# First attention: query and key projections leave PSUM through ScalarE, the rotary products move to GpSimd, and the DMA queue's order changes

## The chip, the cores and the metric

The kernel runs on 1 core of a Trainium2 chip. The metric is the device time of one execution in microseconds (us), the median of several runs. The engines are TensorE (PE in the profile, its weight loads PEld), VectorE (DVE), ScalarE (ACT), GpSimd (POOL) and SyncE (SP, which here only issues DMAs). They run side by side and wait for one another by semaphores.

## The reference

Eight batches of 128 x 256 go through a cross attention, a mixture-of-experts layer, a second cross attention and a low-rank expert layer. The change is in the first attention alone. `b` is 8, `d_model` 128, `n` 256; there are 16 heads of 8 channels.

```python
def apply_cached_rotary_emb(freqs, t):
    return t * freqs[0] + rotate_half(t) * freqs[1]
q = proj(Wq, bq, query).reshape(b, HD, H, n)     # proj: W @ x + bias
k = proj(Wk, bk, key).reshape(b, HD, H, n)
v = proj(Wv, bv, value).reshape(b, HD, H, n)
q = jnp.transpose(apply_cached_rotary_emb(encoding, jnp.transpose(q, (0, 2, 3, 1))), (0, 3, 1, 2))
k = ... the same for k
scores = jnp.einsum('bdhn,bdhm->bhnm', q, k) / np.float32(np.sqrt(HD))
prob = jax.nn.softmax(scores, axis=-1)
x = jnp.einsum('bhnm,bdhm->bdhn', prob, v)
out = jnp.einsum('oi,bin->bon', Wm, x.reshape(b, d_model, n)) + bm[None, :, None]
```

## The kernel before

**Rounds.** The first attention takes one round for each batch b, 0 to 7. A round has eight pairs of heads and two spots for each, spots 0 to 15. At the even spots TensorE makes the scores of the next pair (L679) and, for a batch further on, the same scores once more for their row maxima (L658); spots 3, 7, 11 and 15 multiply probabilities by values (`pv`, L694). Three things of later batches are woven in: the maxima of batch b+1 (pairs 2 to 7 at spots 0 to 10) and of batch b+2 (pairs 0 and 1, spots 12 and 14), the projections of batch b+3 (`q` at spot 1, `k` at spot 5), and the values of b+1 (spot 9).

**The ring.** Projections, maxima, transposed maxima (`maxT`) and values all go through three PSUM banks, used in turn. A use of a bank waits until the use three before it has been taken out. All are taken out by VectorE, in the program's order, which counts `misc_free` up. A pair's maxima need two banks and two VectorE reduces (L1535).

**Projection to scores.** `project` (L643) writes W x and the rotated W x into one bank. VectorE's `factors` (L1524) adds the bias and multiplies by the rotary table, once for each half, into `rope_ab`. GpSimd adds the halves into `qk` (`add_factors`, L454). Scores need full precision from bf16 products, so `qk` is split into three bf16 parts: ScalarE casts the first (`first_parts`, L1140), GpSimd subtracts it (L457), ScalarE casts the second (`second_parts`, L1144), GpSimd subtracts that into the third (`third`, L460). SP writes the parts replicated into a DRAM scratch (`parts_to_dram`, six DMAs), and reads them back as stacks `qstk` and `kstk` (`stack_from_dram`, four DMAs), of which there are three sets.

**Maxima to scores.** When four pairs of a batch (a half) have their maxima, GpSimd negates them and splits them in three (`negate`, six small instructions, L1364 to L1368), TensorE transposes them (`maxT`, L666), VectorE copies them out (L1539), and SP writes them as rows into `qstk` (`rows_at`, L533). The scores of that half wait for these rows. `maxT` stands at spots 6 and 14, ahead of a `pv`, so TensorE, which works in order, holds everything behind it until `negate` is done.

**GpSimd's round**, in order: `divide` of batch b-1; `negate` of half 0; then for batch b+3 the add, the first subtraction, `normalize` of b+4 (L1378), the third part; then `negate` of half 1. In rounds 5 and 6 there is no batch b+3, and no projection, add or parts. ScalarE also does the exponentials (L1133), one for each pair, and in rounds 1 to 4 issues two weight DMAs at pair 1; in rounds 5 and 6 it issues zero fills of 1 MB there.

## Time and profile before

| | us |
|---|---|
| median of 3 runs | 404.87 (400.6 to 405.14) |
| the profiled execution, its own time | 402.56 |
| span in its trace | 400.8 |
| VectorE busy over the span | 290.7 (73%) |
| TensorE busy | 297.2 (74%) |
| ScalarE busy | 166.5 (42%) |
| GpSimd busy | 100.1 (25%) |

The span runs from the first to the last instruction; the rest of an execution's time lies around it. Busy shares are averages over stages with different limits, so the first attention (about 21 to 146 us of the span) has to be read by its rounds. A row of a timeline gives the start, the time to the end of the last instruction in it, the engine, the line, what is written from what, how many instructions were merged, and in brackets the idle time ahead of it with what ended it.

### The profile page before, as it was taken

The numbers are of one execution on the slowest core, as the hardware profiler recorded it, in microseconds if no ns is written. First come the engines' busy times: TensorE is split into PE (matmuls) and PEld (weight loads), VectorE is DVE, ScalarE is ACT, GpSimd is POOL, SyncE is SP. The second block draws the span as 40 slices with busy tenths as digits, with TensorE's granted clock in tenths as the row PEclk, the third lists the DMA queues.
The fourth block names the chain that finished last, engine by engine and source line by source line (L and its number), as shares of the span: only waits on it lengthen the run. The fifth ranks groups of instructions, "written<-read, shape, count | busy, mean of one in ns | idle before, by whom it ended". The sixth has DMA issues, their size and how long they took to land.

```text
span 400.8 us, 7274 instructions
## 1 busy us (share of the span) xinstructions
PE 297.2 (74%) x2650; PEld 187.0 (47%) x2650; DVE 290.7 (73%) x771; ACT 166.5 (42%) x264; POOL 100.1 (25%) x201
## 2 busy tenths in 40 slices
PE   4156978888777668999969998044857696776894
PEld 3122444444434425876648997022534454452453
DVE  6977789989988866769134674275878978776894
ACT  1103376476575565163335664011644545350101
POOL 1234246346343222007701120645000001000000
PEclk9855699999999999599998999555888969698999
DMA  7593447857859451002262775625466564510011
GB/s 249 164 267 101 131 115 218 271 139 222 263 162 265 151 201 61 2 0 90 101 186 79 229 227 194 184 79 144 138 180 182 152 202 141 167 43 0 2 52 52
DMA packets 76387, 58.19 MB, mean 145 GB/s; under 512 B 5056, under 2 KB 73152, under 8 KB 76352
## 3 DMA queue, kind: packets, MB, share of 16 engines
q1 hardware_dynamic: 66688, 42.68, 35.6%
q10 hardware_dynamic: 8128, 10.85, 8.7%
q0 software_dynamic: 1536, 4.20, 3.3%
q8 instruction: 21, 0.34, 0.4%
q14 instruction: 14, 0.11, 0.1%
HBM read 32.87 MB, written 24.64 MB: 143 GB/s over the span
## 4 chain that ended last, share of the span: by engine, by line
PE 37%; DVE 26%; DMA 11%; issue 10%; SPq 5%; ACT 4%; POOL 4%; another core or an unknown queue 1%; DVEq 0%; POOLq 0%
DVE mx L1535 8%; DMA stack_scratch<-parts 5%; PE psum L986 4%; PE psum L694 4%; PE psum L998 3%; PE psum L643 3%; PE psum L856 2%; PE psum L797 2%; PE psum L658 2%; DVE rope_ab L1524 2%; PE psum L811 2%; PE psum L974 2%; PE psum L679 2%; SPq L487 1%; PE psum L1092 1%
## 5 line engine op out<-in xcount | busy, mean ns | idle before, releaser
L1535 DVE TENSOR_REDUCE mx<-psum 128x2 f32<-128x512 f32 x128 | 81.1, 682 | 14.3 <-PE psum L658 12.9
L1133 ACT ACTIVATE prob<-psum 128x1024 f32<-128x1024 f32 x64 | 63.8, 1022 | 41.9 <-PE psum L679 41.9
L1307 ACT ACTIVATE prob<-psum 128x1024 f32<-128x1024 f32 x32 | 32.5, 1023 | 28.0 <-PE psum L946 28.0
L658 PE MATMUL psum<-kstk,qstk 64*128 64x256 bf16 x256 | 27.7, 299 | 22.0 <-DVE mx L1535 12.3
L694 PE MATMUL psum<-prob,vt 128*32 128x256 f32 x512 | 35.9, 392 | 5.3 <-ACT prob L1133 4.2
L460 POOL TENSOR_TENSOR parts<-qk_rest,parts 128x256 bf16<-128x256 f32 (+1 forms) x15 | 13.5, 901 | 66.8 <-ACT parts L1282 63.5
L658 PEld LDWEIGHTS psum<-kstk,qstk 64*128 64x128 bf16 x256 | 9.9, 99 | 35.4 <-DVE mx L1535 24.0
L679 PE MATMUL psum<-qstk,kstk 64*128 64x256 bf16 x256 | 25.2, 282 | 0.3 <-DMA qstk<-mT 0.2
L694 PEld LDWEIGHTS psum<-prob,vt 128*32 128x32 f32 x512 | 16.3, 110 | 13.6 <-ACT prob L1133 6.0
L946 PE MATMUL psum<-qstk,kstk 64*128 64x128 bf16 x256 | 14.2, 240 | 10.8 <-issue 9.8
L962 PE MATMUL psum<-prob,vt 128*32 128x128 f32 x512 | 21.7, 292 | 0.2 <-ACT prob L1307 0.2
L784 PE MATMUL psum<-eye,xn 128*128 128x128 f32 x32 | 8.0, 340 | 15.9 <-DVE xn L1807 11.1
L986 PE MATMUL psum<-xnT,qstk 128*128 128x128 f32 x124 | 17.9, 290 | 2.3 <-DVE xnT L1776 2.2
L1447 POOL DMA_INDIRECT wup<-sorted_y,slots x16 | 15.3, 958 | 15.8 <-issue 15.6
L1076 PE MATMUL psum<-wd,xnT 128*128 128x512 f32 x32 | 16.2, 654 | 3.9 <-DVE xall L1852 3.9
L679 PEld LDWEIGHTS psum<-qstk,kstk 64*128 64x128 bf16 x256 | 8.5, 95 | 20.8 <-issue 13.0
L986 PEld LDWEIGHTS psum<-xnT,qstk 128*128 128x128 f32 x124 | 16.4, 205 | 3.0 <-DVE xnT L1776 2.4
L925 PE MATMUL psum<-wc,xT 128*128 128x256 f32 x32 | 13.7, 571 | 4.8 <-DVE qk_rest L1846 4.2
L946 PEld LDWEIGHTS psum<-qstk,kstk 64*128 64x128 bf16 x256 | 8.4, 103 | 18.6 <-issue 12.7
L1140 ACT CAST parts<-qk 128x512 bf16<-128x512 f32 x8 | 4.9, 617 | 28.8 <-POOL qk L454 17.3
L811 PE MATMUL psum<-wdn,act 128*128 128x256 f32 x64 | 15.2, 381 | 1.5 <-ACT act L1204 1.5
L1524 DVE SCALAR_TENSOR_TENSOR rope_ab<-psum,cols,rope 128x256 f32<-128x256 f32 x32 | 13.6, 469 | 3.4 <-PE psum L643 3.2
(244 smaller groups left out, 621.6 us busy)
## 6 DMA issues: line engine op xcount, KB each, us to landing
qstk<-stack_scratch SPq DMA_DIRECT2D x32, 256.0 KB, 4.2
kstk<-stack_scratch SPq DMA_DIRECT2D x30, 256.0 KB, 4.6
stack_scratch<-parts SPq DMA_DIRECT2D x23, 192.0 KB, 2.1
prob<-sorted_x SPq DMA_DIRECT2D x15, 256.0 KB, 3.2
stack_scratch<-parts SPq DMA_DIRECT2D x25, 128.0 KB, 2.1
sorted_x<-zero_row ACTq DMA_DIRECT2D x3, 1024.0 KB, 5.0
wup<-in_wup ACTq DMA_DIRECT2D x4, 640.0 KB, 4.9
wdn<-in_wdn ACTq DMA_DIRECT2D x4, 640.0 KB, 6.3
```

Of the source, the lines that this page charges most:

```text
L658: last = nc.tensor.matmul(banks[s][:, nb * D:(nb + 1) * D], qstk[par][rows, pair, nb * P:(nb + 1) * P], kstk[par][rows, pair, :], start=Tr ...
L679: last = nc.tensor.matmul(exp_buf(k)[:, s, mb * D:(mb + 1) * D], kstk[b % SETS][rows, k, mb * P:(mb + 1) * P], qstk[b % SETS][rows, k, :], ...
L694: last = nc.tensor.matmul(pv_bank(1)[32 * j:32 * j + 32, g * D:(g + 1) * D], vt[b % 2][:, mb, 4 * t + j, 8:40] if low else vt[b % 2][:, mb ...
L811: last = nc.tensor.matmul(y_banks(c)[:, j // 2, (j % 2) * D:(j % 2 + 1) * D], act2[n % 2][:, j * P:(j + 1) * P], wdn[:, NE + g, :], start= ...
L946: last = nc.tensor.matmul(exp_buf(k)[:, s, at * P:(at + 1) * P], kstk[par][rows, 2 * k + pp, ch * P:(ch + 1) * P], qstk[par][rows, 2 * k + ...
L962: last = nc.tensor.matmul(pv_bank(k // 2)[32 * j:32 * j + 32, g * P:(g + 1) * P], v[:, 8 * k + h, 8:40], prob[k % 2][:, at * P:(at + 1) * ...
L986: last = nc.tensor.matmul(psum[:, n % 2, t_ * P:(t_ + 1) * P], tile_w(n, t_)[:, f * P:(f + 1) * P], tile_xT(n)[:, (2 * t_ + f) * P:(2 * t_ ...
L1076: last = nc.tensor.matmul(psum[:, b % 4, :], xnT[:, f, b * P:(b + 1) * P], wd[:, f, :], start=(f == 0), stop=(f == 1))
L1133: nc.scalar.activation(prob[(b * PAIRS + k) % 3][:], exp_buf(k).rearrange("p a n -> p (a n)"), ACT.Exp, scale=SCALE).then_inc(exp_done, 1)
L1307: nc.scalar.activation(prob[k % 2][:], exp_buf(k).rearrange("p a n -> p (a n)"), ACT.Exp, scale=SCALE).then_inc(exp_done, 1)
L1524: last = nc.vector.scalar_tensor_tensor(out=rope_ab[:, r, ten, :], in0=bank[:, r * D:(r + 1) * D], scalar=cols[:, 2 * ten + r:2 * ten + r ...
L1535: nc.vector.tensor_reduce(mx[:, half, :, 4 * s + p4:4 * s + p4 + 1], bank.rearrange("n (b m) -> n b m", b=2), AX_X, ALU.max).then_inc(misc ...
```

## The change

VectorE's `factors` is gone from the rounds (it stays in the prologue, for batches 0 to 2). Its two instructions for each tensor become two ScalarE activations (`take_turned`, Identity with a bias) from PSUM into `rope_ab`, placed behind the exponentials of pairs 1 and 3, and one GpSimd product for each tensor in place (`turn`). The banks of `q` and `k` are counted by a new semaphore `turned_in`, and TensorE waits for the one or the other (`wait_bank`). `first_parts` moves from pair 4 to pair 5, `second_parts` from pair 5 to pair 6. On GpSimd the third part moves behind `negate` of half 1. SP issues the rows of both halves ahead of the parts.

```diff
+        ALIGNED = max(A_AT[use_] for use_ in A_AT if use_[0] in ("q", "k")) + 1
+        ACT_BANKS = sorted(A_AT[use_] for use_ in A_AT if use_[0] in ("q", "k"))
+        def vector_frees(u):
+            return u + 1 if u >= ALIGNED else u + 1 - len([x for x in ACT_BANKS if x <= u])
+        def wait_bank(eng, u):
+            if u in ACT_BANKS:
+                eng.wait_ge(turned_in, ACT_BANKS.index(u) + 1)
+            else:
+                eng.wait_ge(misc_free, vector_frees(u))
...
             for b in range(5):
                 rows_at(b + 1, 0)
+                rows_at(b + 1, 1)
                 parts_to_dram(b + 3)
-                rows_at(b + 1, 1)
                 for half in range(2):
                     stack_from_dram(b + 3, half)
...
-                pe.wait_ge(misc_free, u - 3 + banks_of(use))
+                for bank_use in range(u - 3, u - 3 + banks_of(use)):
+                    wait_bank(pe, bank_use)
...
+            def take_turned(use, ten):
+                u, b = A_AT[use], use[1]
+                act.wait_ge(misc_full, u + 1)
+                act.wait_ge(qk_ready, b + 1)
+                for r in range(2):
+                    last = nc.scalar.activation(rope_ab[:, r, ten, :], misc(u)[:, r * D:(r + 1) * D], ACT.Identity,
+                                                bias=cols[:, 2 * ten + r:2 * ten + r + 1])
+                last.then_inc(turned_in, 1)
...
-                    if b + 3 < NB and k == 4:
-                        first_parts(b + 3)
+                    if b + 3 < NB and k in (1, 3):
+                        take_turned(("q" if k == 1 else "k", b + 3), k // 3)
                     if b + 1 < NB and k == 5:
                         take_values(b + 1)
                     if b + 3 < NB and k == 5:
+                        first_parts(b + 3)
+                    if b + 3 < NB and k == 6:
                         second_parts(b + 3)
...
+            def turn(b):
+                for ten in range(2):
+                    pool.wait_ge(turned_in, 2 * (b - 3) + ten + 1)
+                    both = rope_ab[:, :, ten, :]
+                    steps.then(nc.gpsimd.tensor_tensor(both, both, rope[:], ALU.mult))
+                add_factors(nc.gpsimd)
...
                 if b + 3 < NB:
-                    rotate(A_AT["k", b + 3] + 1)
+                    turn(b + 3)
                     rest(b + 3, (b + 3) % 2)
                     if b + 4 < NB:
-                        pool.wait_ge(misc_free, PRO_AT["q", 2] + 1 if b == 0 else A_AT["q", b + 2] + 1)
+                        if b:
+                            wait_bank(pool, A_AT["q", b + 2])
                         normalize(b + 4)
-                    third(b + 3, (b + 3) % 2)
                 if b + 1 < NB:
                     negate_at(b + 1, 1)
+                if b + 3 < NB:
+                    third(b + 3, (b + 3) % 2)
...
-                elif kind == "q":
-                    dve.wait_ge(qk_ready, b + 1)
-                    factors(0, bank)
-                elif kind == "k":
-                    factors(1, bank)
```

Once the last `k` is past, one VectorE drain counts `misc_free` up by ten, so that later uses are counted as before.

**GpSimd, from the end of `negate` of half 0 to `negate` of half 1.** Before (L454 is the add, L457 and L460 the subtractions, L1378 `normalize`, L1364 and after it `negate`):

```order
L1368 TENSOR_TENSOR mpart<-mneg,zeros 128x4x4
L454 TENSOR_TENSOR qk<-rope_ab 128x512
L457 TENSOR_TENSOR qk_rest<-qk,parts 128x512
L1378 TENSOR_SCALAR xn<-xall,nmean,rstd 128x256
L460 TENSOR_TENSOR parts<-qk_rest,parts 128x2x256
L1364 TENSOR_TENSOR mneg<-zeros,mx 128x16
```

Now (L1431 are the new products, L469 the add, L472 and L475 the subtractions, L1406 `normalize`, L1392 to L1396 `negate`, L1418 the next round's `divide`):

```order
L1431 TENSOR_TENSOR rope_ab<-rope_ab,rope 128x2x256 x2
L469 TENSOR_TENSOR qk<-rope_ab 128x512
L472 TENSOR_TENSOR qk_rest<-qk,parts 128x512
L1406 TENSOR_SCALAR xn<-xall,nmean,rstd 128x256
L1392 TENSOR_TENSOR mneg<-zeros,mx 128x16
L1394 TENSOR_TENSOR mpart<-mneg,zeros 128x4x4
L1395 TENSOR_TENSOR mneg<-mneg,mpart 128x16
L1394 TENSOR_TENSOR mpart<-mneg,zeros 128x4x4
L1395 TENSOR_TENSOR mneg<-mneg,mpart 128x16
L1396 TENSOR_TENSOR mpart<-mneg,zeros 128x4x4
L475 TENSOR_TENSOR parts<-qk_rest,parts 128x2x256
L1418 TENSOR_TENSOR o<-pvT,den 128x8x16 x2
```

Two products came in ahead of the add, and the third part went behind the negation.

**SP, one batch's parts.** Before (L533 the rows of one half, L487 and L492 the parts, L499 and L500 the stacks' reads):

```order
L533 DMA qstk<-mT 6x4x256
L487 DMA stack_scratch<-parts 128x3x256
L487 DMA stack_scratch<-parts 128x2x256
L487 DMA stack_scratch<-parts 128x256
L492 DMA stack_scratch<-parts 128x768
L492 DMA stack_scratch<-parts 128x512
L492 DMA stack_scratch<-parts 128x256
L533 DMA qstk<-mT 6x4x256
L499 DMA qstk<-stack_scratch 128x4x256
L500 DMA kstk<-stack_scratch 128x4x256
```

Now (L548 the rows, L502 and L507 the parts, L514 and L515 the reads):

```order
L548 DMA qstk<-mT 6x4x256 x2
L502 DMA stack_scratch<-parts 128x3x256
L502 DMA stack_scratch<-parts 128x2x256
L502 DMA stack_scratch<-parts 128x256
L507 DMA stack_scratch<-parts 128x768
L507 DMA stack_scratch<-parts 128x512
L507 DMA stack_scratch<-parts 128x256
L514 DMA qstk<-stack_scratch 128x4x256
L515 DMA kstk<-stack_scratch 128x4x256
```

The rows of half 1, which exist only at the end of a round, stand ahead of the parts of the same round.

## Rows read from the trace of the kernel before

**Rows 1.** The page, busy time of each engine.
```profile
PE 297.2 (74%) x2650; PEld 187.0 (47%) x2650; DVE 290.7 (73%) x771; ACT 166.5 (42%) x264; POOL 100.1 (25%) x201
```

**Rows 2.** Windows, rounds 1 to 5: start:end, length, busy by engine, PEclk, DMA share, GB/s.
```profile
57.40:72.60 15.20, 12.72 (x147) 6.40 (x147) 13.58 (x26) 9.39 (x12) 7.54 (x18) 1.00 0.74 215
72.60:87.80 15.20, 12.72 (x147) 6.39 (x148) 13.58 (x26) 9.39 (x12) 7.56 (x18) 1.00 0.69 202
87.80:103.27 15.47, 12.72 (x147) 6.40 (x148) 13.76 (x27) 9.40 (x12) 7.55 (x18) 1.00 0.73 216
103.27:118.47 15.20, 12.72 (x150) 6.47 (x150) 13.58 (x27) 9.39 (x12) 7.02 (x17) 1.00 0.72 210
118.47:132.45 13.98, 10.13 (x142) 5.28 (x138) 12.04 (x23) 8.19 (x10) 3.42 (x14) 1.00 0.80 229
```

**Rows 3.** Timeline of VectorE in round 4, which starts at 103.27.
```profile
105.48 0.78 DVE L1524 SCALAR_TENSOR_TENSOR rope_ab<-psum,cols,rope 128x256 f32<-128x256 f32 x2
...
108.68 0.88 DVE L1524 SCALAR_TENSOR_TENSOR rope_ab<-psum,cols,rope 128x256 f32<-128x256 f32 x2
...
113.52 3.87 DVE L1535 TENSOR_REDUCE mx<-psum 128x2 f32<-128x512 f32 x6
```

**Rows 4.** Timeline of GpSimd: one row of round 2, then round 4.
```profile
97.59 0.55 POOL L1378 TENSOR_SCALAR xn<-xall,nmean,rstd 128x256 f32<-128x256 f32 x1
...
109.64 1.28 POOL L454 TENSOR_TENSOR qk<-rope_ab 128x512 f32<-128x512 f32 x1 [0.39 <-DVE rope_ab L1524]
111.65 1.15 POOL L457 TENSOR_TENSOR qk_rest<-qk,parts 128x512 f32<-128x512 f32 x1 [0.73 <-ACT parts L1140]
113.61 1.16 POOL L460 TENSOR_TENSOR parts<-qk_rest,parts 128x512 bf16<-128x512 f32 x1 [0.81 <-ACT parts L1144]
114.88 0.22 POOL L1364 TENSOR_TENSOR mneg<-zeros,mx 128x16 f32<-128x16 f32 x1
```

**Rows 5.** Timelines of round 5, without projections: GpSimd, TensorE, VectorE.
```profile
121.98 0.22 POOL L1364 TENSOR_TENSOR mneg<-zeros,mx 128x16 f32<-128x16 f32 x1 [0.37 <-DVE mx L1535]
...
123.47 0.22 POOL L1368 TENSOR_TENSOR mpart<-mneg,zeros 128x16 bf16<-128x16 f32 x1
128.86 0.22 POOL L1364 TENSOR_TENSOR mneg<-zeros,mx 128x16 f32<-128x16 f32 x1 [5.17 <-DVE mx L1535]
...
130.72 0.22 PE L666 MATMUL psum<-eye,mpart 128*24 128x128 bf16 x1 [0.69 <-POOL mpart L1368]
...
127.50 3.87 DVE L1535 TENSOR_REDUCE mx<-psum 128x2 f32<-128x512 f32 x6
...
132.45 1.29 DVE L1535 TENSOR_REDUCE mx<-psum 128x2 f32<-128x512 f32 x2 [0.89 <-PE psum L658]
```

**Rows 6.** Timelines of round 0, TensorE and GpSimd.
```profile
45.97 1.86 PE L643 MATMUL psum<-ctx_all,wa 128*128 128x256 f32 x4
...
53.83 0.22 POOL L1364 TENSOR_TENSOR mneg<-zeros,mx 128x16 f32<-128x16 f32 x1
```

**Rows 7.** Line L454 (ns min/median/max) on VectorE; timeline of GpSimd, the divide.
```profile
L454 DVE TENSOR_TENSOR qk<-rope_ab x1: 692/692/692, 10.5 to 10.5; 128x512 f32<-128x512 f32 x1
...
120.84 0.77 POOL L1390 TENSOR_TENSOR o<-pvT,den 128x128 f32<-128x128 f32 x2 [4.25 <-DVE den L1551]
```

**Rows 8.** Timeline of ScalarE in round 4.
```profile
110.95 0.62 ACT L1140 CAST parts<-qk 128x512 bf16<-128x512 f32 x1 [0.92 <-POOL qk L454]
...
112.65 0.37 ACT L1151 COPY vt<-psum 128x256 f32<-128x256 f32 x1 [0.15 <-PE psum L713]
```

**Rows 9.** Timeline of SP: round 4's parts, their stack read in round 5.
```profile
114.81 1.44 SPq L487 DMA_DIRECT2D stack_scratch<-parts  x3
...
119.04 0.39 SPq L499 DMA_DIRECT2D qstk<-stack_scratch  x1
```

**Rows 10.** A weight DMA (KB each, us to landing); windows, the busiest 10 us of round 4.
```profile
wup<-in_wup ACTq DMA_DIRECT2D x4, 640.0 KB, 4.9
...
103.00:113.00 10.00, 8.79 (x92) 4.40 (x88) 9.23 (x18) 5.99 (x8) 4.53 (x10) 1.00 0.86 248
```

More of the change, by code:

```diff
@@ L228, in build @@
         gap_done = sem("gap_done")
+        turned_in = sem("turned_in")
         egap_done = sem("egap_done")
@@ L536, in rows_at @@
             def rows_at(b, half):
-                max_rows(b, half, A_AT["maxT", b, half] + 1)
+                max_rows(b, half, vector_frees(A_AT["maxT", b, half]))
             sp.wait_ge(fill_out, 16 * 2 * SETS)
@@ L1395, in negate_at @@
             def negate_at(b, half):
-                negate(A_AT["max", b, 4 * half + 3] + 2, half)
+                negate(vector_frees(A_AT["max", b, 4 * half + 3] + 1), half)
+            def turn(b):
[4 more added lines that the diff above has]
+                add_factors(nc.gpsimd)
             rotate(PRO_AT["q", 1] + 1)
@@ L1637, in _ @@
                     for use in a_uses(b, spot):
-                        a_use(use, misc(A_AT[use]), A_AT[use])
+                        if use[0] not in ("q", "k"):
+                            a_use(use, misc(A_AT[use]), A_AT[use])
+                        elif A_AT[use] + 1 == ALIGNED:
+                            nc.vector.drain().then_inc(misc_free, len(ACT_BANKS))
                     if spot == 2 and b == NB - 1:
```

## The prediction

> **What bounds the kernel now.** I read the page's busy times first: VectorE and TensorE stand near three quarters each and GpSimd at a quarter [rows 1], which says little about a stage. So I cut the first attention into rounds, from the first maxima reduce of one to that of the next. Rounds 1 to 4 take 15.20, 15.20, 15.47 and 15.20 us with VectorE busy 13.58 to 13.76 of them; round 5, which has no projection and so none of the work that this change moves, still takes 13.98 [rows 2]. That is the first warning: taking 1.7 us of VectorE away (0.78 + 0.88, [rows 3]) has cut a round by 1.22 us even where GpSimd and TensorE lost their share of the projections too.
>
> Then the timelines, for what ends a round. The first instruction of the second `negate` starts at 114.88 in round 4 and the next round at 118.47, 3.59 later [rows 2, 4]. In round 5 it is 128.86 and 132.45, again 3.59, in detail: six small instructions, `maxT` on TensorE at 130.72 after waiting 0.69 us for GpSimd, `pv`, scores, maxima [rows 5]. So **a round ends 3.59 us after the second `negate` starts**. That start has two gates. One is VectorE: the reduces of pair 7 are the first two of the six that start at 113.52, 1.29 us for two, done at 114.81. The other is GpSimd's own order: the third part ends at 113.61 + 1.16 = 114.77 [rows 3, 4]. Before the change the two gates close within 0.05 us. The change takes work from the one and gives more to the other.
>
> **Part by part.** Offsets are from a round's start.
>
> *VectorE.* Without `factors` the round looks like round 5: reduces of pair 3 end so that the first `negate` starts at 121.98 - 118.47 = 3.51. TensorE still makes the two projections, and the bank order makes the maxima behind a projection wait for both reduces ahead of it, so I put pair 7's reduces at 9.20 (round 5: 127.50 - 118.47 = 9.03 [rows 5]; round 4: 10.25 [rows 3]). VectorE's gate would thus open at 9.20 + 1.29 + 0.07 = 10.56. By this gate alone a round would be 10.56 + 3.59 = 14.15 us.
>
> *ScalarE.* Four activations of 128x256 out of PSUM, each like the copy of values at 0.37 us [rows 8]: at most 1.5 us a round on an engine busy 9.39 of 15.20. The query's pair is due when its projection is in (about 1.1), and its bank is first missed at 3.2; the key's is in at 4.7, taken by about 5.4, and `maxT` behind it is due then. Cost nothing, covered by that slack; if the cover went, it would be 0.3 us a round.
>
> *GpSimd.* First `negate` 3.51 to 5.22 (121.98 to 123.47 + 0.22 [rows 5]). No row shows the product. Its nearest is the add, same size, two fp32 inputs: 1.28 [rows 4]. Bounds: 1.15, the subtraction, and 1.54, four times the divide's 0.77/2 for 128 elements [rows 4, 7]. I take 1.27, since the add differs only in the operation. Then, with 0.1 between instructions without a wait and 0.08 after a wait for the engine itself: products 5.33 and 6.68, add 8.03 to 9.31, ScalarE's cast 9.34 to 9.96 (0.62 [rows 8]), subtraction 10.04 to 11.18, `normalize` 0.55 to 11.73 [rows 4], second `negate` at 11.84. Before it started at 114.88 - 103.27 = 11.61. So **GpSimd's gate is late by 0.23 us, with VectorE's long open**: the add starts 1.66 later (8.03 for 109.64 - 103.27 = 6.37), and the third part, now behind `negate`, gives back 1.43. Rounds 1 to 3 become 11.84 + 3.59 = 15.43: +0.23, +0.23 and -0.04, the last because round 3 held a stall of 0.27 on VectorE, which now has cover. Round 4 has no `normalize`: `negate` at 11.29, 14.88, so -0.32. Sum over these four: +0.10.
>
> The Trainium skill (GPSIMD Engine Reference, section 3.1) says that ordinary elementwise work is about 2 times slower there than on the Vector engine, 4497 ns for a `tensor_tensor` add of 2048 fp32. It speaks against this change. The trace has the same add at 0.69 us on VectorE and 1.28 on GpSimd [rows 4, 7], 1.85 times. A quarter of the page's figure, as an estimate 1.12 us, would make the four rounds about 1.2 us less in sum.
>
> *Round 0.* TensorE is at its slow clock and the key's projection ends at 47.83 [rows 6], so the key's product cannot start before about 48.6. Along the same chain I get the second `negate` at 54.07 for 53.83: +0.24.
>
> *SP and the parts.* The third part now ends at about 14.8, and SP first issues the rows of half 1 (14.5 to 15.2). The six writes go out from 15.2, where before it was 114.81 - 103.27 = 11.54 [rows 9]: 3.7 us later, at the start of the next round instead of ahead of it. There they meet the two weight DMAs of ScalarE, 640 KB each [rows 10]. The reads of the stacks started at 119.04, 4.2 us after the first write [rows 9]; the same lag would now put them at 4.0 into the next round, and with the engines shared I put them at 6. The first half-stack is then in at about 11.4 and all, with the next rows of maxima behind them in the queue, at about 12.8. In a round of 15.43, `maxT` is held until 13.7 anyway, and working back from it the maxima of spot 12 may be as late as 12.2 and the scores of spot 14 as late as 13.1. So nothing in rounds 1 to 4. Round 5 is shorter, its limits 10.75 and 11.7, and the 1 MB zero fill stands where the weights did: **+0.8** (0 to 2.0).
>
> *TensorE's waits.* One more semaphore in front of a few maxima: nothing, or up to 0.05 each on some twelve in the chain, 0.6 at most.
>
> *Sum:* 0.24 + 0.10 + 0.8 = +1.1 us. Nothing after round 5 is touched but one drain. Against the profiled execution's own 402.56 that gives 403.7. The median of the runs shown is 2.3 higher, 404.87, and would give 406.0; the profile is one draw from runs that spread over 4.5 us. I forecast **405.0**, between the two.
>
> **Rivals.** *A, VectorE was the bound and its relief arrives.* Rounds 1 to 4 go to 14.15 and the fourth's stall goes: 1.05 + 1.05 + 1.32 + 1.05 = 4.5, round 0 another 0.2, less the 0.8 in round 5: about -4, so 398.6 to 401 by the two bases, 400. It needs the products to take 0.65 us or less each, as VectorE would do them. For it: round 5's 13.98, and VectorE busy 89% of a round. Against: every GpSimd row of this size is 1.15 or more. Even a round of 13.5 for all five, VectorE's full 1.7 off, would be -8.3, just at 2%.
>
> *B, the later writes hit the DMA engines, and scores wait for stacks and rows.* From a round's start 0.77 MB of parts (12 copies of 64 KB), 1.28 MB of weights and 1.05 MB of stacks (16 of 64 KB) have to pass before the rows of half 0 land. At the 248 GB/s of the busiest stretch [rows 10] this is 12.5 us, and with 1.5 us until the first lands 14.0, against the limit of 13.1: +0.9 in rounds 1 to 4, +2 in round 5, with the rest +5.9, so 408.5 to 410.8. It decides from the point where the rows land later than 13.1 into a round. For it: share 0.86 in that stretch. Against: the weights land in 4.9 us beside the stacks [rows 10], so most of their traffic is past when the reads start. The Trainium skill (DMA: Bandwidth & Descriptors, "Queues, rings and completion order") says that a DMA engine goes round robin between queues packet by packet, and takes one queue's descriptors in order; by it the large weight packets get through beside the small ones of the parts, and the rows stand behind the stacks, which is this rival. No row of before shows the parts and the weights starting together.
>
> *C, the products cost 1.54.* Two times 0.27 a round, five rounds: +2.7, in all +3.8: 406.4 to 408.7.
>
> **Chances.** Forecast 0.60, A 0.12, B 0.16, C 0.12. The range takes in A's upper part and most of B, with the spread of the two bases: 400.0 to 410.0. A measurement of this kernel tells about 2%, 8.1 us, from no change. Faster by that needs all of VectorE's share and more, 0.05; slower needs B and C together with a stall in round 0, 0.07; within 0.88.
>
> **What would show it.** In the profile after, GpSimd's products at 1.27 us; the second `negate` starting at 11.8 in rounds 1 to 3 with no idle ahead of it, its predecessor `normalize`; VectorE idle 1.5 to 3 us ahead of a reduce or the `maxT` copy late in each round, where it had 0.89; rounds of 15.4, 15.4, 15.4, 14.9. Rival A shows as rounds near 14.2 with GpSimd idle ahead of `negate`; B as TensorE waiting at L673 or L694 for `kstk` or `qstk`. Wrong would be: products under 0.7, a cast on ScalarE that finds the engine occupied and starts after 9.4, or reads of the stacks issued after 7 into the round.

## The result, and the profile after

| | before | after |
|---|---|---|
| median of the runs on the same chips, us | 405.0 (400.6 to 410.9, 4 runs) | 426.27 (423.64 to 429.07, 4 runs) |
| ratio to before | | 1.056 (1.044 to 1.069) |
| the profiled execution, us | 402.56 | 427.89 |
| span in its trace, us | 400.8 | 426.0 |
| mean granted TensorE clock of the span | 0.877 | 0.844 |

The kernel became 5.6% slower, about 21 us, where no change was forecast (405.0, range 400 to 410). The two profiled executions are 25.2 us apart in their spans. Some executions of every version come out a few per cent slower than its others; the ratios here leave them out, and of the profiles only that of e3 is of such a one. The page of after, busy time by engine, answers to [rows 1]: VectorE 6.6 us less, ScalarE 8.7 and GpSimd 12.1 us more, as the change says, and TensorE 11.6 us more, though it has the same instructions.

```profile
PE 308.8 (72%) x2650; PEld 193.8 (45%) x2650; DVE 284.1 (67%) x751; ACT 175.2 (41%) x284; POOL 112.2 (26%) x211
```

The windows of rounds 1 to 5 of after (start:end, length, busy by engine, PEclk, DMA share, GB/s) answer to [rows 2].

```profile
57.78:74.76 16.98, 13.98 (x147) 7.18 (x147) 12.26 (x23) 11.06 (x16) 9.95 (x20) 0.90 0.60 181
74.76:92.73 17.97, 14.40 (x147) 7.45 (x147) 12.25 (x22) 11.06 (x16) 9.95 (x20) 0.88 0.60 178
92.73:110.73 18.00, 14.04 (x147) 7.19 (x148) 12.24 (x22) 10.85 (x16) 9.95 (x20) 0.90 0.59 177
110.73:130.59 19.86, 14.67 (x150) 7.41 (x150) 12.34 (x22) 11.26 (x16) 9.40 (x19) 0.83 0.54 161
130.59:151.17 20.58, 12.18 (x142) 6.12 (x138) 12.14 (x23) 8.21 (x10) 3.42 (x14) 0.83 0.62 193
```

The first starts 0.38 us later than before. The five then take 93.39 us for 75.05, so 18.3 of the 25.2 us arise here. VectorE is relieved (12.25 for 13.58) and nothing comes of it. Two columns point to why: the granted clock was 1.00 in all five rounds before and is 0.83 to 0.90 now, and the DMA share fell to 0.54 to 0.62 from 0.69 to 0.80, so the DMA engines too stand idle for a larger part of a round.

The waits of after between 40 and 170 us (waiting engine and tile, releaser, us in total, times, longest) begin the search. VectorE's wait for the scores of the maxima was 10.4 us before (40 to 146 us), and TensorE had no wait for a DMA there at all:

```profile
DVE mx L1573 <- PE psum L673: 37.4, 37, 5.3
...
PE psum L673 <- DMA kstk<-stack_scratch: 11.7, 5, 4.7
```

TensorE waits five times for the key's stack, once in each round, and six times for the rows of maxima (8.8 us in all, the first of them in round 0). Its timeline in rounds 1, 2, 4 and 5 shows both:

```profile
69.21 0.39 PE L673 MATMUL psum<-kstk,qstk 64*128 64x256 bf16 x4 [0.86 <-DMA kstk<-stack_scratch]
71.45 0.39 PE L694 MATMUL psum<-qstk,kstk 64*128 64x256 bf16 x4 [1.84 <-DMA qstk<-mT]
...
87.19 0.40 PE L673 MATMUL psum<-kstk,qstk 64*128 64x256 bf16 x4 [1.85 <-DMA kstk<-stack_scratch]
89.02 0.39 PE L694 MATMUL psum<-qstk,kstk 64*128 64x256 bf16 x4 [1.43 <-DMA qstk<-mT]
...
126.53 0.61 PE L694 MATMUL psum<-qstk,kstk 64*128 64x256 bf16 x4 [1.69 <-DMA qstk<-mT]
...
145.55 0.61 PE L673 MATMUL psum<-kstk,qstk 64*128 64x256 bf16 x4 [4.70 <-DMA kstk<-stack_scratch]
147.20 0.61 PE L694 MATMUL psum<-qstk,kstk 64*128 64x256 bf16 x4 [1.04 <-DMA qstk<-mT]
...
148.35 1.91 PE L709 MATMUL psum<-prob,vt 128*32 128x256 f32 x13
```

The last row is the second half of the effect. Thirteen matmuls of `pv` that took 1.03 us before take 1.91 after the stall. The windows of round 5 of after, during the stall and behind it:

```profile
140.00:145.00 5.00, 0.85 (x16) 0.15 (x8) 0.92 (x2) 1.14 (x2) 1.32 (x6) 0.91 1.04 329
...
148.00:151.00 3.00, 3.00 (x31) 1.66 (x30) 1.48 (x3) 1.03 (x2) 0.00 (x0) 0.52 0.00 0
```

For 5 us TensorE is busy 0.85 us while the DMA engines are full; then it works without a gap at a granted clock of 0.52, the lower level (1.2 GHz of 2.4), and the next round starts only behind this work.

Where the bytes came to lie is on the timeline of SP (the time behind the start is that of issuing). It answers to [rows 9]:

```profile
56.44 1.77 SPq L502 DMA_DIRECT2D stack_scratch<-parts  x3
58.25 1.63 SPq L507 DMA_DIRECT2D stack_scratch<-parts  x3
65.25 0.37 SPq L514 DMA_DIRECT2D qstk<-stack_scratch  x1
...
67.32 7.01 SPq L548 DMA_DIRECT2D qstk<-mT  x2
74.44 1.44 SPq L502 DMA_DIRECT2D stack_scratch<-parts  x3
...
138.59 0.37 SPq L514 DMA_DIRECT2D qstk<-stack_scratch  x1
```

and on that of ScalarE's queue:

```profile
57.36 0.64 ACTq L1194 DMA_DIRECT2D wup<-in_wup  x1
58.04 0.61 ACTq L1195 DMA_DIRECT2D wdn<-in_wdn  x1
...
139.10 0.40 ACTq L1188 DMA_DIRECT2D sorted_x<-zero_row  x1
```

The parts' writes (56.44 to 59.88) and the weights (57.36) start together. The reads, which wait for the last write, are issued 8.5 to 9.7 us after the first write (8.8 in the rows above); before it was 4.2 to 6.3. SP's own waits for the landing of the parts, before (50 to 125 us) and after (50 to 145), five times each:

```profile
SPq L499 <- DMA stack_scratch<-parts: 5.2, 5, 2.0
...
SPq L514 <- DMA stack_scratch<-parts: 23.7, 5, 6.2
```

In round 5 the read at 138.59 meets a second transfer, the 1 MB zero fill at 139.10: the fills of rounds 5 and 6 stand at pairs 1 and 6, not at pair 1 alone.

### The profile page after: what moved, and what is told of

It reads as the page before. It is cut to its first block, busy times and chain, and to the rows that moved or that the text cites. A ratio compares the mean times of both kernels' runs of the same rounds, so it can differ in the third digit from the quotient of the medians.

```text
span 426.0 us, 7337 instructions
## 1 busy us (share of the span) xinstructions
PE 308.8 (72%) x2650; PEld 193.8 (45%) x2650; DVE 284.1 (67%) x751; ACT 175.2 (41%) x284; POOL 112.2 (26%) x211
## 4 chain that ended last, share of the span: by engine, by line
PE 42%; DMA 19%; DVE 18%; SPq 9%; issue 7%; ACT 3%; POOL 2%; DVEq 0%; POOLq 0%
DMA stack_scratch<-parts 7%; DMA qstk<-mT 6%; PE psum L709 5%; PE psum L1002 4%; PE psum L813 3%; PE psum L1014 3%; PE psum L658 3%; DVE mx L1573 3%; PE psum L827 3%; PE psum L694 3%; PE psum L673 2%; PE psum L872 2%; SPq L502 2%; SPq L507 2%; PE psum L1108 2%
## 5 line engine op out<-in xcount | busy, mean ns | idle before, releaser
L1573 DVE TENSOR_REDUCE mx<-psum 128x2 f32<-128x512 f32 x128 | 82.0, 683 | 40.9 <-PE psum L673 40.4
L673 PE MATMUL psum<-kstk,qstk 64*128 64x256 bf16 x256 | 29.7, 313 | 30.9 <-DMA kstk<-stack_scratch 21.1
L709 PE MATMUL psum<-prob,vt 128*32 128x256 f32 x512 | 40.0, 426 | 4.4 <-ACT prob L1149 4.1
L694 PE MATMUL psum<-qstk,kstk 64*128 64x256 bf16 x256 | 26.8, 296 | 9.0 <-DMA qstk<-mT 9.0
L475 POOL TENSOR_TENSOR parts<-qk_rest,parts 128x256 bf16<-128x256 f32 (+1 forms) x15 | 13.5, 898 | 69.9 <-ACT parts L1310 68.5
L673 PEld LDWEIGHTS psum<-kstk,qstk 64*128 64x128 bf16 x256 | 11.8, 104 | 43.2 <-issue 22.2
L709 PEld LDWEIGHTS psum<-prob,vt 128*32 128x32 f32 x512 | 18.1, 117 | 12.9 <-ACT prob L1149 5.6
L978 PE MATMUL psum<-prob,vt 128*32 128x128 f32 x512 | 22.9, 304 | 0.2 <-ACT prob L1335 0.2
L1418 POOL TENSOR_TENSOR o<-pvT,den 128x128 f32<-128x128 f32 x16 | 6.2, 406 | 52.7 <-DVE den L1589 52.7
L1092 PE MATMUL psum<-wd,xnT 128*128 128x512 f32 x32 | 17.3, 690 | 3.2 <-DVE xall L1888 3.2
L962 PEld LDWEIGHTS psum<-qstk,kstk 64*128 64x128 bf16 x256 | 8.3, 102 | 20.1 <-issue 11.5
L978 PEld LDWEIGHTS psum<-prob,vt 128*32 128x32 f32 x512 | 13.5, 118 | 6.7 <-issue 4.5
L1014 PE MATMUL psum<-wdn,act 128*128 x62 | 16.1, 381 | 0.0
```

Of the source, the lines that this page charges most:

```text
L673: last = nc.tensor.matmul(banks[s][:, nb * D:(nb + 1) * D], qstk[par][rows, pair, nb * P:(nb + 1) * P], kstk[par][rows, pair, :], start=Tr ...
L694: last = nc.tensor.matmul(exp_buf(k)[:, s, mb * D:(mb + 1) * D], kstk[b % SETS][rows, k, mb * P:(mb + 1) * P], qstk[b % SETS][rows, k, :], ...
L709: last = nc.tensor.matmul(pv_bank(1)[32 * j:32 * j + 32, g * D:(g + 1) * D], vt[b % 2][:, mb, 4 * t + j, 8:40] if low else vt[b % 2][:, mb ...
L962: last = nc.tensor.matmul(exp_buf(k)[:, s, at * P:(at + 1) * P], kstk[par][rows, 2 * k + pp, ch * P:(ch + 1) * P], qstk[par][rows, 2 * k + ...
L978: last = nc.tensor.matmul(pv_bank(k // 2)[32 * j:32 * j + 32, g * P:(g + 1) * P], v[:, 8 * k + h, 8:40], prob[k % 2][:, at * P:(at + 1) * ...
L1014: last = nc.tensor.matmul(psum[:, 2 + n % 2, t_ * D:(t_ + 1) * D], act2[n % 2][:, t_ * P:(t_ + 1) * P], w, start=True, stop=True)
```

## The experiments

All ratios are to the kernel before, on the same chip. Of the trace of each, "rounds" are the lengths of rounds 1 to 5; before has 15.20, 15.20, 15.47, 15.20, 13.98 and after 16.98, 17.97, 18.00, 19.86, 20.58. The theory is that of rival B, the traffic. Its own rival is that the products on GpSimd, or the later `negate`, cost the time.

### e5_before_rows_first

The kernel before, with only SP's order changed:

```diff
                 rows_at(b + 1, 0)
+                rows_at(b + 1, 1)
                 parts_to_dram(b + 3)
-                rows_at(b + 1, 1)
```

> The kernel before, with only SP's order changed: the rows of both halves ahead of the parts. Nothing moves between engines. If the order alone is the cause: the parts wait for the rows of half 1 at the end of each round, the rounds are 17 to 20 as in the change, and the time is +15 to +22 us, 420 to 427. If the longer GpSimd chain is the cause: within 2 us of the kernel before.

Measured: 422.74 us (420.23 to 425.29), ratio 1.046 (1.035 to 1.056). Rounds 17.74, 17.11, 18.20, 18.68, 19.51. Two lines moved on a queue give +5%, most of what the whole change does, with no product on GpSimd and nothing on ScalarE. TensorE in this kernel waits for the same two tiles in each round, here in round 2:

```profile
88.72 0.39 PE L658 MATMUL psum<-kstk,qstk 64*128 64x256 bf16 x4 [2.22 <-DMA kstk<-stack_scratch]
89.42 0.39 PE L679 MATMUL psum<-qstk,kstk 64*128 64x256 bf16 x4 [0.30 <-DMA qstk<-mT]
```

Its third part is ready at 85.48 + 1.16 = 86.64 and its writes are issued only at 92.69: the rows of half 1 ahead of them hold a finished product for 6 us. In after both moves make the parts late, and SP's order is the smaller share: in round 1 the third part is ready at 70.99 + 1.15 = 72.14 and its writes go out at 74.44. That is 16.7 us into the round, where it was 11.5 before; 2.8 of the 5.1 us come from the third part's place behind `negate`, 2.3 from the rows ahead on SP.

### e4_third_first

The other half alone: the change on the engines, but the third part ahead of the second `negate` again and SP in the order of before.

```diff
                 rows_at(b + 1, 0)
-                rows_at(b + 1, 1)
                 parts_to_dram(b + 3)
+                rows_at(b + 1, 1)
...
+                if b + 3 < NB:
+                    third(b + 3, (b + 3) % 2)
                 if b + 1 < NB:
                     negate_at(b + 1, 1)
-                if b + 3 < NB:
-                    third(b + 3, (b + 3) % 2)
```

> Only the moves between engines: the activations on ScalarE, the products on GpSimd and the later casts stay, the third part is again ahead of the second negate and SP's order is that of the kernel before. Theory (GpSimd's chain sets a round's end, DMA traffic is as before): the second negate starts 1.4 us later than in the change (11.5 into a round), at 13.0, so rounds 1 to 3 take 16.6, round 4 about 16.0, round 5 stays at 14.0, TensorE waits for maxT's negate and not for kstk or rows. In all +6 against the kernel before, 410 to 412. If moving the work to GpSimd and ScalarE were what costs the 20 us, it would be at 420 or more; if VectorE's relief arrived, below 403.

Measured: 418.41 us (414.27 to 419.31), ratio 1.035 (1.026 to 1.043), above what was expected. Rounds 17.82, 17.72, 17.88, 17.96, 13.98, and no wait of TensorE for a DMA in them. So on the engines alone the change costs too, unless the third part gives way. GpSimd and TensorE, round 2 (starts at 78.40):

```profile
82.75 0.22 POOL L1392 TENSOR_TENSOR mneg<-zeros,mx 128x16 f32<-128x16 f32 x1 [1.20 <-DVE mx L1573]
...
92.12 0.22 POOL L1392 TENSOR_TENSOR mneg<-zeros,mx 128x16 f32<-128x16 f32 x1
```

```profile
93.98 0.22 PE L681 MATMUL psum<-eye,mpart 128*24 128x128 bf16 x1 [2.63 <-POOL mpart L1396]
...
95.45 0.64 PE L673 MATMUL psum<-kstk,qstk 64*128 64x256 bf16 x4
```

GpSimd's chain from the first `negate` to the second is 9.37 us, with no idle ahead of the last. A round at full clock would be 3.51 + 9.37 + 3.59 = 16.5. But TensorE stands for 2.63 us ahead of `maxT`, and in the window 94 to 98 its granted clock was 0.63: maxima at 0.64 us for 0.39. So the first `negate` of this round starts at 4.35 instead of 3.51 and the tail is 4.00 instead of 3.59: 4.35 + 9.37 + 4.00 = 17.72, the round measured. The slow clock adds 1.25 us here and, by the same sum, 1.4 to 1.5 in rounds 1, 3 and 4, where it lies mostly in the tail (4.37 to 4.94). The idle ahead of `maxT` (2.63 to 2.68) returns in each round, and the lower clock with it. Round 0 pays too: round 1 starts at 60.58, 3.2 us later than before.

### e3_parts_first

After, with SP's order of before only (the first piece of the diff of e4).

> The change, with SP's order as before it (rows of half 0, parts, rows of half 1), weights and zero fills where they were. Collision theory: the parts are then issued as soon as the third part is done, 14.4 us into a round where the change issued them at 16.7 to 18, still just ahead of the weights; the reads start about 2.3 to 3 us earlier and most of the waits for kstk (0.9 to 2.9) and rows in rounds 1 to 4 go: rounds of 15.3 to 16.5, -6 to -9 us. Round 5 loses about 2 of its 6.6. Feedback theory, a form of lateness (the rows of half 1 stand ahead of the parts, so a late maxT makes the next parts later still): the rounds stop growing from one to the next (17.0, 18.0, 18.0, 19.9) and are equal within 0.5. If the order of SP does not matter: within 2 us of the change.

Measured: 426.07 us (418.84 to 426.68, 4 runs), without a ratio, so whether it gains anything on after stays open; the 6 to 9 us that were expected are not seen. Its rounds 20.34, 20.37, 20.21, 19.71, 17.42 are read for the place of the wait alone. The rows of half 1, small as they are, now stand behind the late parts, and a pair of scores at spot 6 waits 3 to 4 us in each round:

```profile
65.32 0.61 PE L694 MATMUL psum<-qstk,kstk 64*128 64x256 bf16 x4 [3.89 <-DMA qstk<-mT]
```

With the third part behind `negate` and the weights at pair 1, neither order of SP is free: in the one TensorE waits for stacks and rows late in a round, in the other for rows early in it.

### e1_weights and e2_weights_zeros

Is it the weights that the writes run into? e1 is after with the weights at pair 4; e2 has the zero fills in round 6 alone besides.

```diff
-                    if 1 <= b <= 4 and k == 1:
+                    if 1 <= b <= 4 and k == 4:
                         inner_weights(CHUNK * (b - 1))
```

and in e2 also

```diff
-                    if b in (5, 6) and k in (1, 6):
-                        first = 16 * (b - 5) + 8 * (k // 6)
+                    if b == 6 and k in (1, 3, 5, 7):
+                        first = 4 * (k - 1)
```

> The change, with the two weight DMAs of rounds 1 to 4 issued behind the exponential of pair 4 (some 5.5 us into a round) instead of pair 1, so that they no longer start together with the six writes of the parts. Collision theory: the writes land in about 3 us as in the kernel before, the stacks' reads start 3 to 4 us into the next round instead of 7.5 to 9.6, and TensorE no longer waits for kstk or the rows in rounds 1 to 4. Rounds 1 to 4 go from 17.0, 18.0, 18.0, 19.9 to about 15.1 each, -12 us; round 5 keeps its zero fills and most of its 20.6. In all -11 to -14 against the change, 413 to 416. Lateness theory (the writes are simply issued too late in SP's order, whoever shares the engines): the reads start later than 6 us, rounds stay above 17, less than 4 us gained.

> As the run with later weights, and all four zero fills in round 6 (pairs 1, 3, 5, 7), in which no stack is written or read. Collision theory: round 5 goes from 20.6 to about 14, so another -6 us: 407 to 409, about the kernel before plus 2 at most. Lateness theory: round 5 stays above 18.

Measured: e1 425.1 us (421.33 to 430.51), 1.051 (1.038 to 1.063); e2 418.51 us (416.31 to 420.56), 1.036 (1.027 to 1.045), both some 10 us above what was expected. Rounds of e1 19.53, 16.73, 20.31, 16.14, 21.17, of e2 19.21, 19.36, 19.19, 18.89, 14.00. Round 5 came down to 14.00 in e2, so the zero fills are what made that round 6.6 us longer. Rounds 1 to 4 stayed at 19 us in e2. The first half of the expectation held: in round 1 of e1 the reads are issued 1.3 us after the last write was (63.05 behind 60.36 + 1.42), where in after it was 5.4. But the weights meet the reads and the rows of maxima instead, and TensorE waits for the rows (or, in rounds 1 and 4 of e2, for the key's stack). In round 2 of e2 the rows of half 0 are issued at 84.23, 2.0 us after the first weight, and the scores that need them start 8 us later:

```profile
92.48 0.61 PE L694 MATMUL psum<-qstk,kstk 64*128 64x256 bf16 x4 [4.51 <-DMA qstk<-mT]
```

### e11_quiet_rounds, e12_quiet_norm_later and the control e13_before_quiet

So all of that traffic was taken out: weights at pairs 0, 2, 4, 6 of round 6, zero fills at the same pairs of round 7. e12 also puts `normalize` of b+4 behind the second `negate`. e13 is the kernel before with the weights and zero fills moved as in e11.

```diff
-                    if 1 <= b <= 4 and k == 1:
-                        inner_weights(CHUNK * (b - 1))
-                    if b in (5, 6) and k in (1, 6):
-                        first = 16 * (b - 5) + 8 * (k // 6)
+                    if b == 6 and k % 2 == 0:
+                        inner_weights(CHUNK * (k // 2))
+                    if b == 7 and k % 2 == 0:
+                        first = 4 * k
```

and in e12 also

```diff
-                    if b + 4 < NB:
-                        if b:
-                            wait_bank(pool, A_AT["q", b + 2])
-                        normalize(b + 4)
                 if b + 1 < NB:
                     negate_at(b + 1, 1)
+                if b + 4 < NB:
+                    if b:
+                        wait_bank(pool, A_AT["q", b + 2])
+                    normalize(b + 4)
```

> The change, with all four pairs of weight DMAs issued in round 6 (pairs 0, 2, 4, 6) and the four zero fills in round 7, so that rounds 0 to 5 hold only the parts, the stacks and the rows. The runs with the weights moved to pair 4 only moved the collision from the writes to the reads and the rows behind them. Traffic theory (in a round's time the writes, the reads and the weights must all pass before the rows of half 0, which queue behind the reads): without the weights the rows land by 10.5 into a round, no wait for kstk or rows is left, rounds 1 to 3 take 15.1, round 4 14.6, round 5 14.0; 18 us less than the change up to round 6, 404 to 409 in all. Lateness theory (the writes start too late in themselves): rounds stay above 17 and the time above 418.

> As the run with quiet rounds, and normalize of batch b+4 (0.55 us) put behind the second negate on GpSimd. If GpSimd's chain from the first negate to the second is what sets a round once the DMAs are out of the way, rounds 1 to 3 shorten by 0.5 to 14.6, round 4 stays, 1.5 us in all: 402.5 to 407. If VectorE or TensorE sets it, nothing moves.

> Control: the kernel before with the same move of the weights and zero fills to rounds 6 and 7. There the writes land before the weights start, so both theories expect rounds 1 to 5 as before (15.2, 15.2, 15.2 to 15.5, 15.2, 14.0) and a time within 3 us of it. If the stage behind the attention has to wait for the later weights, that shows here as 1 to 5 us more behind round 7.

| | us | ratio | rounds 1 to 5 |
|---|---|---|---|
| e11 | 408.17 | 1.013 (1.006 to 1.021) | 16.11, 15.17, 16.49, 14.58, 13.98 |
| e12 | 403.74 | 1.0005 (0.997 to 1.004) | 14.58, 14.59, 14.58, 14.58, 13.99 |
| e13 | 406.16 | 1.001 (0.996 to 1.006) | 15.20, 15.20, 15.45, 15.21, 13.98 |

With the bytes gone 4.3 of the 5.6% are gone, and the kernel before gains nothing by the same move. That is the main evidence for the traffic theory: the same weights and zero fills cost the old order nothing and the new one most of its loss. e11 also shows the prediction's own forecast for a round, 15.43, standing free: 15.17 where the clock held. In its rounds 1 and 3 it did not, though nothing was later:

```profile
72.10 0.22 PE L681 MATMUL psum<-eye,mpart 128*24 128x128 bf16 x1 [1.34 <-DVE mx L1573]
...
72.22 1.59 PE L709 MATMUL psum<-prob,vt 128*32 128x256 f32 x13
...
88.27 0.22 PE L681 MATMUL psum<-eye,mpart 128*24 128x128 bf16 x1 [1.31 <-POOL mpart L1396]
...
88.37 1.03 PE L709 MATMUL psum<-prob,vt 128*32 128x256 f32 x13
```

An idle of 1.34 us was followed by the slow clock (0.65 in the window 71.5 to 75), one of 1.31 was not (1.00). In e12 the idle ahead of `maxT` is 0.81 at most and the clock was 1.00 in all five rounds. Its rounds 1 to 3 are 4.0 us shorter than those of e11: three times the 0.56 us of `normalize`, and for the rest the clock. The medians are 4.4 us apart.

### e14_quiet_no_product

e11 with GpSimd's products left out, so the rotated query and key are not multiplied by the table:

```diff
                     both = rope_ab[:, :, ten, :]
-                    steps.then(nc.gpsimd.tensor_tensor(both, both, rope[:], ALU.mult))
```

> The changed kernel with weights and zero fills out of rounds 1 to 5 (as in e11_quiet_rounds), and GpSimd's two products left out of the computation. It asks where the other gate stands, VectorE's, which the prediction put at 14.15 us for rounds 1 to 4. If GpSimd's order is what ended the rounds of e11 (15.17 and 16.49 in the middle) and VectorE's gate is where the prediction put it, rounds come down to 14.0 to 14.3, GpSimd idle ahead of the second negate and VectorE's maxima named as what ended the idle. If the 14.58 of e12_quiet_norm_later was already VectorE's or TensorE's own pace, rounds stay at 14.5 to 14.7 here. Time 401 to 404 us by the first, 403 to 405 by the second.

Measured: 406.61 us over all 8 runs, where before had 406.53 on that chip; ratio 0.996 (0.988 to 1.005), not told from before. Rounds 16.34, 14.70, 14.70, 14.29, 15.22. The rounds of 14.7 are those of the second expectation, but its reason was not. The 2.6 us of products gone shorten round 2 by 0.5 us only, because another wait takes their place. GpSimd, round 3:

```profile
98.58 1.16 POOL L472 TENSOR_TENSOR qk_rest<-qk,parts 128x512 f32<-128x512 f32 x1 [2.47 <-ACT parts L1156]
```

ScalarE's cast stands behind its pair 5 and is not ready earlier. (Round 1, 16.34, holds a wait of 1.91 us for the rows with the slow clock behind it, and round 5 waits of 0.56 for the key's stack and 1.50 for the rows: with no other large transfer in these rounds the rows still come close to too late.) VectorE's gate was not reached in this run.

### e17_gap_late and e18_gap_early

The last question is whether a version can have both. e17 is after with `normalize` behind the second `negate` (as in e12), the weights back in rounds 1 to 4 but at pair 6, and the zero fills spread; e18 has the weights at pair 5.

```diff
+            ZERO_AT = [(5, 5), (6, 1), (6, 6), (7, 1)]
...
-                    if 1 <= b <= 4 and k == 1:
+                    if 1 <= b <= 4 and k == 6:
                         inner_weights(CHUNK * (b - 1))
-                    if b in (5, 6) and k in (1, 6):
-                        first = 16 * (b - 5) + 8 * (k // 6)
+                    if (b, k) in ZERO_AT:
+                        first = 8 * ZERO_AT.index((b, k))
```

> The changed kernel with normalize of batch b + 4 behind the second negate on GpSimd, the weights back in rounds 1 to 4 but issued at pair 6 (9.7 us into a round of 14.58, when the stacks' reads and the rows of half 0 are over and the next parts not yet written), and the zero fills at pair 5 of round 5, 1 and 6 of round 6, 1 of round 7. By the traffic theory only bytes in flight together with the parts' writes, the stacks' reads and the rows of half 0 cost anything: rounds 1 to 4 at 14.6 to 15.0, round 5 at 14.0 to 14.5, rounds 6 and 7 at 12.6 and 11.2 again, so 2 to 4 us less than e12 and than before: 399 to 402 us. If instead any 1.28 MB in a round of 14.6 pushes the queue's work past its limits, TensorE waits for qstk behind the rows as in e1_weights and the rounds go to 16 and over: 408 to 416 us.

> As e17_gap_late, with the weights at pair 5 (7.2 us into the round), while the last stacks' reads and the rows of half 0 behind them are still in flight. In e12, with no weights at all, TensorE still waited 1.05 us for those rows in round 2. By the traffic theory the wait for the rows grows to 2 to 4 us in rounds 1 to 4, each followed by TensorE's lower clock: rounds 16 to 18 us, 408 to 416 us in all. If the order on the queues does not matter and only the number of bytes in a round does, this run and e17_gap_late come out within 2 us of each other.

Measured: e17 403.53 us (398.71 to 410.82, 12 runs) where before had 406.53 over all its runs, ratio 0.994 (0.988 to 0.9995); e18 414.33 us (405.8 to 418.36, 4 runs), too scattered for a ratio, so that of it only the trace is used. The windows of rounds 1, 4 and 5 of e17:

```profile
58.58:73.17 14.59, 12.61 (x147) 6.48 (x148) 12.23 (x22) 10.96 (x16) 9.98 (x20) 1.00 0.71 218
...
102.38:116.98 14.60, 12.73 (x150) 6.54 (x150) 12.32 (x23) 10.95 (x16) 9.44 (x19) 1.00 0.70 218
116.98:131.69 14.71, 10.25 (x142) 5.37 (x138) 12.13 (x22) 8.54 (x10) 3.44 (x14) 1.00 0.64 200
```

The bytes of a round are those of after, and the rounds are as short as with none. SP and ScalarE's queue in round 3 show the gap that was used:

```profile
92.14 0.37 SPq L514 DMA_DIRECT2D qstk<-stack_scratch  x1
...
94.81 7.28 SPq L548 DMA_DIRECT2D qstk<-mT  x2
102.21 1.45 SPq L502 DMA_DIRECT2D stack_scratch<-parts  x3
```

```profile
96.98 0.56 ACTq L1195 DMA_DIRECT2D wup<-in_wup  x1
```

The weights start 2.2 us behind the rows of half 0 and have 5.2 us until the next writes. In e18 they start one pair earlier, at 64.79 in round 1, and TensorE waits for the rows again:

```profile
70.75 0.39 PE L694 MATMUL psum<-qstk,kstk 64*128 64x256 bf16 x4 [2.31 <-DMA qstk<-mT]
```

Its rounds are 16.90, 14.57, 15.41, 15.34, 18.21. So 2.1 us of difference in the issue of 1.28 MB make rounds 1 to 4 up to 2.3 us longer; round 2 shows that a wait of 1.24 us can also cost nothing. Round 5 has no weights in either kernel, and there the order of events is not followed up: the stack's first read is issued 6.6 us into it in e18 and 4.0 in e17, and TensorE waits 3.60 us for the rows where it waits 1.72 in e17. e17 is the one version here whose interval lies below before, by 0.05% to 1.2%. That is below the 2% that would let one call it faster: it is no slower than before, and perhaps slightly faster.

## Why the prediction was wrong

**What held.** The engine terms did. GpSimd's two products took 2.62 us (predicted 2.6) and the add 1.26 (1.28):

```profile
62.97 2.62 POOL L1431 TENSOR_TENSOR rope_ab<-rope_ab,rope 128x512 f32<-128x512 f32 x2
65.67 1.26 POOL L469 TENSOR_TENSOR qk<-rope_ab 128x512 f32<-128x512 f32 x1
...
69.32 0.22 POOL L1392 TENSOR_TENSOR mneg<-zeros,mx 128x16 f32<-128x16 f32 x1
```

The second `negate` started 11.54, 11.55 and 11.54 into rounds 1 to 3 (predicted 11.84), with no idle ahead and `normalize` in front of it. The estimate from the Trainium skill's figure (GPSIMD Engine Reference, section 3.1; a quarter of it, 1.12 us) was 0.14 us low for the add of this size. ScalarE's activations took 0.84 for two, 0.47 each where 0.37 was said, and were covered, as said. VectorE's gate was put at 10.56; in e12 the reduces ahead of the second `negate` end at 96.66 + 1.28 = 97.94, 10.64 into the round. The rule that a round ends 3.59 after the second `negate` held where the clock did: 3.58 in e12 (98.30 to 101.88), 3.59 in round 2 of e11.

**The step that failed** is the one on SP and the parts: "So nothing in rounds 1 to 4", and +0.8 for round 5. In its place the runs showed +18.3 us in rounds 1 to 5. Two parts of it were wrong, and for round 5 a third.

*The transfers.* The reads were put at 6 into the round; they are issued at 7.5, 8.2, 8.0, 9.6 and 8.0, later than the 7 that the prediction had named as a sign of being wrong. The writes left where it had them, 0.1 to 0.7 us ahead of rounds 2 to 5 (predicted 0.2) and 1.3 ahead of round 1. What was wrong is the lag from the first write to the first read. Its 4.2 us was the shortest of five rows of before (6.3, 5.6, 4.8, 4.3, 4.2), and the 2 us put on top for the shared engines were too few: the lag became 8.5 to 9.7. The argument against rival B was that the weights would be past when the reads start, having landed in 4.9 us. That is the first of the two weight transfers only; the page of before has the second beside it:

```profile
wdn<-in_wdn ACTq DMA_DIRECT2D x4, 640.0 KB, 6.3
```

It is issued 0.6 us behind the first, so in after, where they start at 57.36, the weights are in flight for some 7 us, and the reads wait for writes that share the engines with them. Between 55 and 75 us the writes of 192, 128 and 64 KB land in 2.7, 5.3 and 5.2 us by the median, for 2.1, 2.1 and 2.5 before, while the weights take 5.2 and 6.6, for 5.2 and 6.5. The Trainium skill's round robin between queues (DMA: Bandwidth & Descriptors, "Queues, rings and completion order") was in the text as the reason for rival B. The trace fits it, though it doesn't show the turns themselves: whichever of SP's transfers is beside the weights is late, writes in after, reads and rows in e1 and e2, and the weights are not.

*The limits.* Rival B put the landing of the rows at 14.0 by bytes and bandwidth. The scores behind them start at 13.67, 14.26, 14.45, 15.80 and 16.61 into the round, so for rounds 1 to 3 that was right to 0.5 us. But it priced it by the limit of 13.1 for the scores of spot 14 at +0.9, and the rounds grew by 1.78, 2.77 and 2.53. The limit was worked back at full clock. After a stall, TensorE ran at granted clocks of 0.50 to 0.66 in the windows taken, and `maxT` to the next round takes 2.77 us (71.99 to 74.76) where it took 1.73 [rows 5]. With both terms the sum nearly closes: the scores come 0.57, 1.16 and 1.35 us behind the limit in rounds 1 to 3 and the tails are 1.04, 1.37 and 0.85 longer, together 1.6, 2.5 and 2.2, and these rounds exceed the 15.43 that was forecast by 1.55, 2.54 and 2.57. That second microsecond in every round is what neither the forecast nor rival B had; e4 shows it with no wait for a DMA in it at all. At an idle near 1.3 us the runs don't tell whether it comes (e11).

*The second fill.* In round 5 the prediction saw the zero fill of pair 1 only. With the reads 8.0 us into the round the one of pair 6 starts beside them (138.59 and 139.10), and without the fills the round is 14.00 (e2) for 20.58. Why round 4 takes 19.86 where rounds 2 and 3 take 18.0 is not settled: its lag of 9.7 us is the longest of the five, with writes and weights started as in the others.

**The rivals.** Rival C is out (1.31 a product), and so is A: VectorE's relief arrived, but no round came near 14.15. Rival B was given 0.16 and was the mechanism; with e5 showing late parts by the order on SP alone at +17.5 us, and e11 showing what is left without the traffic at 4.7 us above the kernel before on its chip (1.3% by the ratio, with the clock's share in it), it was most of the result. It stood at 408.5 to 410.8 because the late rows were priced at full clock, and because the second zero fill of round 5 was not in it. The range ended inside that span, at 410.0.

What stays open: 6.5 us of the 25.2 between the two profiled executions lie behind round 5, in code that the change doesn't touch. The last stretch of the traces makes up 3.2 of it (114.0 us from 312 on, for 110.8 from 290, at a granted clock of 0.85 for 0.89). The medians are 21 us apart, so part of it is the draw of the two executions; which part is not settled. Nor was a case run in which VectorE's gate alone ends a round.

## What to carry to other kernels

A step that moves later on a DMA queue has to be followed over the round's end: what it starts beside, how long the whole of that is in flight and not only its first transfer, and what stands behind it in the same queue. When a chain of TensorE work is short of slack, price a stall twice, once for the idle time and once for the lower clock behind it, and ask whether the next round meets it again. And where big transfers that nobody waits for share the DMA engines with small ones that somebody does, look for the gap in the critical traffic before moving either: in e17 other places for the weights and zero fills, with `normalize` out of the way, turned 5.6% slower into no slower than before.

## What the runs showed of the hardware

- The granted clock fell to its lower level behind an idle of TensorE of 1.34 us in rounds 1 and 3 of e11 and not behind 1.31 in round 2; in e4 it did behind each of 2.63 to 2.68, in e12 not behind waits of 1.26 and 1.05. No length of one idle separates the cases: it did not fall behind a wait of 2.22 (e5, round 2) or 2.53 (e1, round 4), and behind 1.15 ahead of `maxT` in round 0 it fell in after and not in e3. Work behind it is up to 1.8 times longer: 13 matmuls of `pv` 1.91 us for 1.03.
- A 12 KB write of rows, issued 2.0 us after a weight transfer of 640 KB on another queue and behind four stack reads on its own, let its reader start 8 us later (e2, 84.23 to 92.48), after a wait of 4.51 us.
- Writes of 64 and 128 KB that start beside 1.28 MB of weights land in 5.2 and 5.3 us for 2.5 and 2.1, and the weights in 5.2 and 6.6 for 5.2 and 6.5 (after and before, 55 to 75 us).
- Moving 1.28 MB of weights by one pair, about 2.1 us, changed the rounds that hold them by 0 to 2.3 us (e17 and e18).
- GpSimd multiplies and adds 128x512 fp32 at the same price, 1.31 and 1.26 us; ScalarE takes 128x256 fp32 out of PSUM with a bias in 0.47 us where the plain copy took 0.37 (after).
